# Routed experts of a two-layer block: the plain weight is loaded one slot later, and the vector engine's work inside a slot is put in another order

## The chip, the cores and the metric

The kernel runs on one core of a Trainium2 chip. The metric is the device time of one execution in microseconds; the time before is the median of three runs. TensorE (PE) does the matrix products, VectorE (DVE) and ScalarE (ACT) the element-wise work, GpSimd (POOL) and SyncE (SP) mostly start transfers (DMAs).

## The reference, cut to what matters

Two layers work on 4096 tokens of width 256. The second ends with a routed feed-forward block of 8 experts, and beside it with a mixture of four linear scans whose weights come from the top two of four gate logits (a rank, a top value and a sigmoid for each token):

```python
top_idx = jnp.argmax(gate_logits, axis=-1)
for e in range(NUM_EXPERTS):                       # 8 experts, D_FF = 1024
    mask = (top_idx == e)[..., None]
    h = relu(x @ w1[e] + b1[e])
    y = h @ w2[e] + b2[e]
    out = out + mask * y
...
top_vals, top_idx = jax.lax.top_k(x @ gate_W, 2)   # weights of the scan mixture
weights = softmax(top_vals)
```

The change touches only how this routed block, and the ranks of the last mixture, are put in order.

## The kernel before, in words

Products are made of float32 numbers split into a rounded high part and a low part: `mm3` does three products (high by high, high by low, low by high). Every operand therefore needs a high part (ACT, a copy in the rounded type) and a low part (DVE, a subtraction).

Tokens are sorted by expert into blocks of 128 rows in DRAM. The routed stage then runs over 23 slots in 8 rounds. A round has three slots, k = 0, 1 and 2: two "big" ones of 256 rows with split weights, and a "small" one of 128 rows (`small(k)`), whose first layer takes the plain float32 weight `w1_small` and the plain rows `sT_small`. The last round has only the two big slots. Round 0 and round 7 are written out, rounds 1 to 6 are a hardware loop. Below, slot (r, k) is slot k of round r.

What each engine does in a slot n:

- PE: layer 1 (`L393` to `L395` in a big slot, `L1581` in a small one) fills four PSUM banks q = 0..3, two of the eight column blocks in each; then layer 2 (`L1597` to `L1599`) sums over j = 0..7. Layer 2 waits, for each pair of j, for the low part `eT_l` of that pair (`e_ok`), at j = 0 and 4 for the halves of the low part of w2 (`w2_lo`), and at its start for `ys_ok`, that is, until the sums of the slot before have been taken out of PSUM. Layer 1 of a small slot waits for both halves of `w1_small` (`w1s_in`).
- ACT: for each q, `relu` (two instructions, L1675) and `round_e` (the high part, L1683); between them the high parts of the weights (`w1_half` L1652, `w2_half` L1659) and of the rows (L1663).
- DVE, function `slot` at the end of the file: `rows_out` of the slot before (bias added, L2071; it waits for that slot's last matmul and for its bias `b2b`), `low_e` for each q (L2062), the low parts of the weights (`w1_half` L2035, `w2_half` L2056) and of the rows (L2051), and the turning of the next rows (`turn_rows` L2045). In the first slot of the last round it also has, behind each `low_e`, one `mixture_rank` (L500 to L506), and at the end of the last slot `mixture_top` (L513 to L517) and `mixture_finish`.
- SP, function `slot` of the first block: a queue, in program order, of `store_y` (L1413), the second half of the next w2 (`raw2_half`, L1399, issued when DVE has made the low part of the half that is overwritten), `load_b2` (L1417), in slot 0 of rounds 1 to 6 both halves of `w1_small` (`load_w1_small`, L1392), `load_b1` (L1407), the next w1 (`raw1_half`, L1385, also behind the low parts; both halves in k = 0, one in k = 1 and one in k = 2), and the first half of the w2 after the next. The raw weights have one buffer each.
- POOL loads the rows of later slots (L1811), on a queue of its own.

Of the kernel before, what the change touches and what calls it, by code (L numbers as in the profile page):

```python
# [44 lines left out]
ST = SLOT // P  # L45
# [3 lines left out]
ROUND = 3  # L49
# [15 lines left out]
def build(nc, a, out):  # L65
# [484 lines left out]
    def zero(g):  # L550
        return isinstance(g, int) and g == 0
# [119 lines left out]
    def left(r, k):  # L671

        return NSLOT - 1 - ROUND * r - k if isinstance(r, int) else NSLOT
# [10 lines left out]
    with nc.Block("all") as block:  # L684
# [626 lines left out]
        def _(sp):  # L1311
# [76 lines left out]
            def load_w1_small(r, e):  # L1388
                if not zero(r):
                    wait_alone(sp, l1_full, FJ // 2 * ROUND * r)  # L1390
                for h in (0, 1):
                    sp.dma_start(w1_small[:, :, h * HALF1:(h + 1) * HALF1],  # L1392
                                 a["w1"][bass.ds(e, 1), h].rearrange("a p c f -> p (a c) f")).then_inc(w1s_in, 16)
# [8 lines left out]
            def load_b1(n, k, e):  # L1402
                if not (isinstance(n, int) and n < ROUND):
                    wait_alone(sp, t_ok, FJ * (n - ROUND + 1))
                if not zero(n):
                    wait_alone(sp, b1_in, 16 * n)
                sp.dma_start(b1c[:, k % ROUND, :], a["b1"][bass.ds(e, 1)].rearrange("a p j -> p (a j)")).then_inc(b1_in, 16)  # L1407

            def store_y(r, k):

                wait_alone(sp, ys_ok, ROUND * r + k + 1)
                b, st = blocks(r, k)
                sp.dma_start(y_v[bass.ds(b, st)].rearrange("b p d -> p b d"), y_sb[:, 0:st, :]).then_inc(y_st, 16)  # L1413

            def load_b2(e):

                sp.dma_start(b2b[:], a["b2"][bass.ds(e, 1)].to_broadcast((P, D))).then_inc(b2_in, 16)  # L1417
# [3 lines left out]
            def expert_at(r, o):  # L1421

                if o not in ahead:
                    ahead[o] = expert(ROUND * r + o)
                return ahead[o]

            def slot(r, k):

                n = ROUND * r + k
                if k == 0:  # L1430
                    ahead.clear()
                if not zero(n):
                    store_y(*((r, k - 1) if k else (r - 1, ROUND - 1)))
                if left(r, k) > 0:
                    raw2_half(n + 1, 1, expert_at(r, k + 1))
                load_b2(expert_at(r, k))
                if left(r, k) > 1 and k == 0 and not zero(r):
                    load_w1_small(r, expert_at(r, ST))
                if left(r, k) > 1:
                    load_b1(n + 2, k + 2, expert_at(r, k + 2))  # L1440
                if not small(k) and bigs_left(r, k) > 1:
                    e = expert_at(r, k + ROUND)
                    raw1_half(bigs(r, k) + ST, 0, e)
                    if k == 0:
                        raw1_half(bigs(r, k) + ST, 1, e)
                if small(k):
                    raw1_half(bigs(r, k - 1) + ST, 1, expert_at(r, k - 1 + ROUND))
                if left(r, k) > 1:
                    raw2_half(n + 2, 0, expert_at(r, k + 2))
# [385 lines left out]
        def _(dve):  # L1835
# [238 lines left out]
            def first_halves():  # L2074
# [7 lines left out]
                low_e(0, 3, SLOT)  # L2082
                w1_half(1, 0)

            def low_halves(r, k):

                n, (_, st) = ROUND * r + k, blocks(r, k)
                for q in range(FJ // 2):
                    low_e(n, q, st * P)
                    if left(r, k) == 1:  # L2090
                        mixture_rank(dve, link, mix2, q)
                    if q == 2 and not small(k):
                        for ahead in range(k + 1, next_big(k) + 1):
                            if left(r, k) > 0:
                                turn_rows(r, ahead)
                    if q == 0 and k == 0:
                        w2_half(n, 1)
                    if q == (2 if k == 0 else 1) and not small(k) and bigs_left(r, k) > 0:
                        w1_half(bigs(r, k) + 1, 0)

            def slot(r, k):
                n, (_, st) = ROUND * r + k, blocks(r, k)
                if not zero(n):
                    rows_out(*((r, k - 1) if k else (r - 1, ROUND - 1)))
                if not zero(n) and k > 0:
                    w2_half(n, 1)
                if zero(n):
                    first_halves()
                else:
                    low_halves(r, k)  # L2110
                if left(r, k) > 0:
                    if not small(k):
                        rows_lo(r, next_big(k))
                    if not small(k) and bigs_left(r, k) > 0:
                        w1_half(bigs(r, k) + 1, 1)
                    w2_half(n + 1, 0)
                if left(r, k) == 0:
                    mixture_top(dve, link, mix2)
                    mixture_finish(dve, link, mix2, 2)

            g = GROUPS - 1
# [86 lines left out]
```

## Time and profile before

| | |
|---|---|
| median of 3 runs | 1025.59 us (1025.57 to 1028.11) |
| the profiled execution | 1028.48 us, of which the span is 1026.8 us |
| routed stage, on PE | 645.40 to 881.44 us of the span, 236.0 us |
| granted PE clock | 1.00 |

The span is what the profile covers, from the first to the last instruction; all times of rows are from its start.

### The profile page before, as it was taken

The page shows a single profiled execution, that of the slowest core. Times are in us where ns is not written, and L with a number is a line of the kernel's source. Part 1 is how long each engine was busy: PE and PEld are TensorE (multiplying, and loading weights), DVE is VectorE, ACT ScalarE, POOL GpSimd, SP SyncE. Part 2 cuts the span into 40 slices and gives each one's busy share as a digit, 9 for nine tenths or more (in the row PEclk, how much of TensorE's full clock was granted, in tenths as well). Part 3 has the DMA queues.
Part 4 walks back from the last instruction along what each step waited for, and adds up shares of the span by engine and source line. Part 5 has one row for each costly group of instructions (what it writes and reads, how often), then busy time and mean ns, then how long its engine had stood idle before and what let it go on. Part 6 is the DMA issues. An engine that isn't in the chain of part 4 may idle for free.

```text
span 1026.8 us, 20067 instructions
## 1 busy us (share of the span) xinstructions
PE 1016.7 (99%) x6432; PEld 908.7 (88%) x6432; DVE 793.2 (77%) x1307; ACT 626.2 (61%) x1179; POOL 373.9 (36%) x376
## 2 busy tenths in 40 slices
PE   8999999999999999999999999999999999999998
PEld 7988989989898988989877888999999999888887
DVE  6876767667685777969789998977788778588887
ACT  4554445535444454555566667888889888566665
POOL 3443443444444453443552775122122110482000
PEclk9999999999999999999999999999999999999999
DMA  6226313122132221442546376688897885652203
GB/s 190 69 83 221 103 41 82 55 79 70 41 82 82 81 82 62 144 165 63 194 157 245 116 286 221 199 249 250 267 286 249 284 262 182 230 178 68 92 11 102
DMA packets 112130, 152.12 MB, mean 148 GB/s; under 512 B 40720, under 2 KB 80656, under 8 KB 111056
## 3 DMA queue, kind: packets, MB, share of 16 engines
q1 hardware_dynamic: 100368, 132.35, 39.3%
q0 software_dynamic: 6016, 13.51, 4.5%
q10 hardware_dynamic: 5696, 5.64, 1.7%
q8 instruction: 26, 0.43, 0.2%
q14 instruction: 24, 0.20, 0.1%
HBM read 109.20 MB, written 42.27 MB: 148 GB/s over the span
## 4 chain that ended last, share of the span: by engine, by line
PE 86%; DVE 4%; DMA 3%; issue 3%; SPq 2%; ACT 2%; DVEq 0%; POOL 0%; ACTq 0%; POOLq 0%
PE ps L395 17%; PE ps L393 17%; PE ps L394 17%; PE ps L1194 6%; PE ps L1195 6%; PE ps L1196 6%; DMA raw<-w 2%; PE ps L1597 2%; PE ps L1598 2%; PE ps L1599 2%; PE ps L1212 2%; PE ps L1213 2%; PE ps L1214 2%; PE ps L1263 1%; PE ps L1256 1%
## 5 line engine op out<-in xcount | busy, mean ns | idle before, releaser
L827 POOL TENSOR_TENSOR acc<-acc,ytmp 128x512 f32<-128x512 f32 x120 | 157.7, 1314 | 243.3 <-ACT ytmp L918 223.4
L1637 ACT ACTIVATE act_o<-ps,scan_bias 128x512 f32<-128x512 f32 x189 | 129.5, 688 | 98.1 <-PE ps L395 94.1
L918 ACT ACTIVATE ytmp<-ps,sel 128x256 f32<-128x256 f32 x256 | 107.3, 471 | 95.7 <-PE ps L1196 95.1
L995 DVE SCALAR_TENSOR_TENSOR hT_l<-ps,hT_h 128x512 fp32r<-128x512 f32 (+1 forms) x136 | 88.4, 655 | 87.7 <-ACT hT_h L878 87.6
L1194 PE MATMUL ps<-vals_h,hT_h 128*128 128x256 f32 x512 | 144.9, 283 | 0.1
L1195 PE MATMUL ps<-vals_l,hT_h 128*128 128x256 f32 x512 | 143.8, 281 | 0.0
L1196 PE MATMUL ps<-vals_h,hT_l 128*128 128x256 f32 x512 | 143.5, 280 | 0.0
L878 ACT ACTIVATE hT_h<-ps 128x512 fp32r<-128x512 f32 x128 | 76.3, 596 | 89.4 <-PE ps L395 84.9
L1811 POOL DMA_DIRECT2D rows<-xs_d x92 | 52.8, 575 | 175.2 <-DVE sT L2045 163.8
L1980 DVE TENSOR_TENSOR_SCAN h_b<-a_b,hstate,xs_b 128x512 f32<-128x512 f32 x63 | 88.1, 1398 | 28.2 <-ACT a_b L1644 24.8
L1040 DVE SCALAR_TENSOR_TENSOR acc<-ps,sel,acc 128x256 f32<-128x256 f32 x240 | 104.0, 475 | 3.0 <-PE ps L1196 2.9
L1194 PEld LDWEIGHTS ps<-vals_h,hT_h 128*128 128x128 f32 x512 | 96.5, 188 | 6.4 <-issue 0.8
L1195 PEld LDWEIGHTS ps<-vals_l,hT_h 128*128 128x128 f32 x512 | 96.2, 188 | 4.6
L1196 PEld LDWEIGHTS ps<-vals_h,hT_l 128*128 128x128 f32 x512 | 97.0, 189 | 0.0
L393 PE MATMUL ps<-xT_h,keys_h 128*128 128x512 f32 x240 | 96.7, 403 | 0.0
L395 PE MATMUL ps<-xT_h,keys_l 128*128 128x512 f32 x240 | 94.9, 395 | 0.0
L394 PE MATMUL ps<-xT_l,keys_h 128*128 128x512 f32 x240 | 94.7, 395 | 0.0
L1597 PE MATMUL ps<-w_h,eT_h 128*128 128x256 f32 x312 | 89.8, 288 | 3.9 <-DVE eT_l L2062 3.0
L1598 PE MATMUL ps<-w_l,eT_h 128*128 128x256 f32 x312 | 88.1, 282 | 0.0
L1599 PE MATMUL ps<-w_h,eT_l 128*128 128x256 f32 x312 | 87.9, 282 | 0.0
L395 PE MATMUL ps<-x1T,WB_late 128*128 128x512 f32 (+2 forms) x198 | 77.6, 392 | 0.0
L1675 ACT ACTIVATE t<-ps,b1c 128x256 f32<-128x256 f32 (+1 forms) x184 | 70.0, 431 | 11.1 <-DMA b1c<-b 6.9
(261 smaller groups left out, 2769.6 us busy)
## 6 DMA issues: line engine op xcount, KB each, us to landing
raw<-w SPq DMA_DIRECT2D x78, 512.0 KB, 5.4
x1T<-xT_d SPq DMA_DIRECT2D x16, 512.0 KB, 5.5
comb_b<-comb_d SPq DMA_DIRECT2D x8, 1024.0 KB, 8.5
xn_d<-xn SPq DMA_DIRECT2D x15, 512.0 KB, 2.9
w_small<-w SPq DMA_DIRECT2D x14, 512.0 KB, 5.1
xs_d<-zeros ACTq DMA_DIRECT2D x1, 4992.0 KB, 19.5
x_d<-x SPq DMA_DIRECT2D x8, 512.0 KB, 4.5
xT_d<-nT_h SPq DMA_DIRECT2D x8, 512.0 KB, 2.7
```

Source lines behind the costliest of these rows:

```text
L393: pe.matmul(dst, wh, xh, start=start, stop=False)
L394: pe.matmul(dst, wh, xl, start=False, stop=False)
L395: return pe.matmul(dst, wl, xh, start=False, stop=stop)
L827: pool.tensor_tensor(dst[:, 2:4, :], acc[:, 2:4, :], ytmp[:, k % 2, :, :], ALU.add).then_inc(acc23, 1)
L918: act.activation(ytmp[:, k % 2, j - 2, :], yb(k, j), ACT.Copy, scale=sel[:, j, k:k + 1]).then_inc(y_23, 1)
L1194: pe.matmul(yb(k, j), hT_h[:, k % 2, s], vals_h[:, k, :], start=True, stop=False)
L1195: pe.matmul(yb(k, j), hT_h[:, k % 2, s], vals_l[:, k, :], start=False, stop=False)
L1196: last_mm = pe.matmul(yb(k, j), hT_l[:, k % 2, s], vals_h[:, k, :], start=False, stop=True)
L1597: pe.matmul(dst, eT_h[:, j, t], w2_h[:, j, :], start=j == 0, stop=False)
L1598: pe.matmul(dst, eT_h[:, j, t], w2_l[:, j, :], start=False, stop=False)
L1599: last_mm = pe.matmul(dst, eT_l[:, j, t], w2_h[:, j, :], start=False, stop=j == FJ - 1)
L1637: act.activation(act_o[:, i % 2, w, :], ps[:, 3 * (i % 2) + w, :], func, bias=scan_bias[:, w, i:i + 1]).then_inc(act_g, 1)
```

## The change

In the queue of SP: the plain weight `w1_small` is loaded in slot k = 1 of rounds 1 to 6, behind `load_b1`, and no longer in slot k = 0; in a small slot `load_b2` comes ahead of the second half of w2, in the big slots it stays behind it. On DVE: in slots k = 0 the sums of the slot before (`rows_out`) are taken out behind the first `low_e`, no longer ahead of it; in small slots `w2_half(n, 1)` comes behind the first `low_e`, no longer ahead of it. The four `mixture_rank` of the last mixture move from slot (7, 0) to the slots (0, 1) (behind its last `low_e`) and (0, 2) (behind its last three), and `mixture_top` from the end of slot (7, 1) to the end of slot (0, 2).

```diff
@@ -1431,13 +1431,16 @@
                     ahead.clear()
                 if not zero(n):
                     store_y(*((r, k - 1) if k else (r - 1, ROUND - 1)))
+                if small(k):
+                    load_b2(expert_at(r, k))
                 if left(r, k) > 0:
                     raw2_half(n + 1, 1, expert_at(r, k + 1))
-                load_b2(expert_at(r, k))
-                if left(r, k) > 1 and k == 0 and not zero(r):
-                    load_w1_small(r, expert_at(r, ST))
+                if not small(k):
+                    load_b2(expert_at(r, k))
                 if left(r, k) > 1:
                     load_b1(n + 2, k + 2, expert_at(r, k + 2))
+                if left(r, k) > 0 and k == 1 and not zero(r):
+                    load_w1_small(r, expert_at(r, ST))
                 if not small(k) and bigs_left(r, k) > 1:
                     e = expert_at(r, k + ROUND)
                     raw1_half(bigs(r, k) + ST, 0, e)
@@ -2082,27 +2085,31 @@
                 low_e(0, 3, SLOT)
                 w1_half(1, 0)
 
+            RANKS2 = [(1, 3), (2, 1), (2, 2), (2, 3)]
+
             def low_halves(r, k):
 
                 n, (_, st) = ROUND * r + k, blocks(r, k)
                 for q in range(FJ // 2):
                     low_e(n, q, st * P)
-                    if left(r, k) == 1:
-                        mixture_rank(dve, link, mix2, q)
+                    if zero(r) and (k, q) in RANKS2:
+                        mixture_rank(dve, link, mix2, RANKS2.index((k, q)))
                     if q == 2 and not small(k):
                         for ahead in range(k + 1, next_big(k) + 1):
                             if left(r, k) > 0:
                                 turn_rows(r, ahead)
                     if q == 0 and k == 0:
+                        rows_out(r - 1, ROUND - 1)
+                    if q == 0 and k != 1:
                         w2_half(n, 1)
                     if q == (2 if k == 0 else 1) and not small(k) and bigs_left(r, k) > 0:
                         w1_half(bigs(r, k) + 1, 0)
 
             def slot(r, k):
                 n, (_, st) = ROUND * r + k, blocks(r, k)
-                if not zero(n):
-                    rows_out(*((r, k - 1) if k else (r - 1, ROUND - 1)))
                 if not zero(n) and k > 0:
+                    rows_out(r, k - 1)
+                if k == 1:
                     w2_half(n, 1)
                 if zero(n):
                     first_halves()
@@ -2114,8 +2121,9 @@
                     if not small(k) and bigs_left(r, k) > 0:
                         w1_half(bigs(r, k) + 1, 1)
                     w2_half(n + 1, 0)
+                if zero(r) and small(k):
+                    mixture_top(dve, link, mix2)
                 if left(r, k) == 0:
-                    mixture_top(dve, link, mix2)
                     mixture_finish(dve, link, mix2, 2)
```

## Rows read from the trace of the kernel before

**Rows 1.** The page: busy time by engine, and the chain by engine.

```profile
PE 1016.7 (99%) x6432; PEld 908.7 (88%) x6432; DVE 793.2 (77%) x1307; ACT 626.2 (61%) x1179; POOL 373.9 (36%) x376
...
PE 86%; DVE 4%; DMA 3%; issue 3%; SPq 2%; ACT 2%; DVEq 0%; POOL 0%; ACTq 0%; POOLq 0%
```

**Rows 2.** Busy time by stretch: slot k = 1 of rounds 1, 3, 5.

```profile
687.04:700.14 13.10, 11.71 (x99) 11.51 (x97) 9.21 (x13) 9.91 (x18) 1.93 (x4) 1.00 0.90 287
...
749.12:760.50 11.38, 11.38 (x98) 11.38 (x97) 9.92 (x14) 10.20 (x18) 2.76 (x5) 1.00 0.97 319
...
809.14:820.59 11.45, 11.45 (x99) 11.45 (x98) 9.45 (x13) 10.16 (x18) 2.17 (x4) 1.00 0.97 327
```

**Rows 3.** Busy time by stretch: slot k = 2 of rounds 0, 1; sum of all seven.

```profile
668.36:675.34 6.98, 6.69 (x58) 6.53 (x57) 5.11 (x8) 5.38 (x15) 2.51 (x5) 1.00 0.73 206
700.14:707.16 7.02, 6.71 (x59) 6.52 (x57) 5.10 (x8) 5.06 (x14) 2.74 (x5) 1.00 0.71 199
...
sum 48.49, PE 47.19 PEld 45.73 DVE 34.76 ACT 38.63 POOL 15.95; mean PE 6.74 PEld 6.53 DVE 4.96 ACT 5.52 POOL 2.28
```

**Rows 4.** Busy time by stretch: slot k = 0 of rounds 5, 6, 7.

```profile
797.44:809.14 11.70, 11.70 (x99) 11.52 (x98) 8.52 (x11) 9.99 (x18) 2.21 (x4) 1.00 0.78 249
827.37:839.37 12.00, 11.72 (x99) 11.51 (x97) 8.49 (x11) 10.48 (x18) 2.21 (x4) 1.00 0.74 243
857.64:870.05 12.41, 11.65 (x98) 11.45 (x97) 10.37 (x24) 9.93 (x17) 0.00 (x0) 1.00 0.56 174
```

**Rows 5.** PE in order of time: start, duration, line, idle before with releaser.

```profile
697.16 0.38 PE L1597 MATMUL ps<-w_h,eT_h 128*128 128x256 f32 x1 [1.39 <-DVE eT_l L2062]
...
704.19 0.38 PE L1597 MATMUL ps<-w_h,eT_h 128*128 128x256 f32 x1 [0.31 <-DVE eT_l L2062]
...
868.52 0.39 PE L1597 MATMUL ps<-w_h,eT_h 128*128 128x256 f32 x1 [0.76 <-DVE eT_l L2062]
```

**Rows 6.** ACT in order of time, slots (1, 1), (1, 2) and (6, 0).

```profile
693.86 1.06 ACT L1652 ACTIVATE w_h<-raw 128x1024 fp32r<-128x1024 f32 x1 [2.28 <-DMA raw<-w]
...
701.39 0.60 ACT L1675 ACTIVATE t<-ps,b1c 128x128 f32<-128x128 f32 x2
...
704.91 0.42 ACT L1683 ACTIVATE eT_h<-t 128x256 fp32r<-128x256 f32 x1
...
830.86 1.07 ACT L1659 ACTIVATE w_h<-raw 128x1024 fp32r<-128x1024 f32 x1 [0.19 <-DMA raw<-w]
```

**Rows 7.** SP's queue in order of time: the plain weight, w1, and three loads of b1.

```profile
683.65 2.74 SPq L1392 DMA_DIRECT2D w_small<-w  x2
...
688.27 1.43 SPq L1385 DMA_DIRECT2D raw<-w  x2
...
692.85 0.33 SPq L1407 DMA_DIRECT2D b1c<-b  x1
...
754.73 0.33 SPq L1407 DMA_DIRECT2D b1c<-b  x1
...
814.05 0.33 SPq L1407 DMA_DIRECT2D b1c<-b  x1
```

**Rows 8.** DMA issues at 692.87:692.97: size, us from issue to landing.

```profile
b1c<-b SPq DMA_DIRECT2D x1, 4.0 KB, 6.0
```

**Rows 9.** DMA issues at 754.75:754.85, the same columns.

```profile
b1c<-b SPq DMA_DIRECT2D x1, 4.0 KB, 7.1
```

**Rows 10.** DMA issues at 814.07:814.17, the same columns.

```profile
b1c<-b SPq DMA_DIRECT2D x1, 4.0 KB, 5.7
```

**Rows 11.** DVE in order of time: small slot (1, 2), and ranks in slot (7, 0).

```profile
702.50 1.22 DVE L2056 TENSOR_TENSOR w_l<-raw,w_h 128x1024 fp32r<-128x1024 f32 x1
703.63 1.19 DVE L2062 TENSOR_TENSOR eT_l<-t,eT_h 128x256 fp32r<-128x256 f32 x3
...
863.75 0.17 DVE L504 TENSOR_TENSOR cmp<-logits 128x8 f32<-128x8 f32 x1
...
864.60 0.69 DVE L2062 TENSOR_TENSOR eT_l<-t,eT_h 128x512 fp32r<-128x512 f32 x1
```

## The prediction

> **What bounds the kernel now.** I read the page first: PE is busy for 99% of the span and makes up 86% of the chain that ended last [rows 1]. So an edit to the order of DVE's and SP's work can only pay where PE stands still, or cost where it makes PE stand still. I then cut the routed stage into its slots and read each stretch by itself. PE works there at one matmul of 256 columns in about 0.118 us (rows 2: the second slot of round 5 has its 96 in 11.45 us, that of round 3 in 11.38 us, with PE busy all the way). At this rate a big slot is worth 11.4 us, and a small one 32 plain products of 0.11 us and 24 of 0.118 us, 6.4 us. The 23 slots would need 16 x 11.4 + 7 x 6.4 = 227 us and take 236. All that can be won in this stage is thus 9 us, 0.9% of the time, and the timeline says where it lies:
>
> - Slot (1, 1) takes 13.10 us, 1.7 over the floor [rows 2]. PE waits there for 1.39 us for `eT_l` in the middle of layer 2 [rows 5]; behind that wait is ACT, which stood for 2.28 us until the first half of w1 had landed [rows 6]. That half was issued at 688.27, behind two plain weight transfers whose issue at 683.65 took 2.74 us [rows 7].
> - The seven small slots take 48.5 us together, 3.7 over their floor, each between 6.8 and 7.1 [rows 3]. Layer 2 starts late, on `eT_l` [rows 5], because DVE first does the 1.22 us of `w2_half` and only then `low_e` [rows 11].
> - The slots k = 0 of rounds 1 to 5 take about 11.7 us, that of round 6 takes 12.00 and that of round 7 takes 12.41 [rows 4]; in the last PE waits for 0.76 us for an `eT_l` [rows 5] that stands behind the ranks of the mixture.
>
> The other view that matters is the DMA share, the column before the last of rows 2 to 4: 0.78 in the slot k = 0 of round 5, about 0.7 in small slots, but 0.97 in the slots k = 1 of rounds 3 and 5. The load that the change moves goes from the first of these stretches into the one that is full.
>
> **The change, part by part.**
>
> *The plain weight leaves slot 0.* Its two halves no longer stand ahead of b1 and of the first half of w1. In round 1 the w1 half can be issued some 3 us earlier (it then waits only for the low part of the old w1), so the 2.28 us of ACT [rows 6] and the stall they cause go: 13.10 to 11.6, **-1.5 us**. The slots k = 1 of the other rounds have no stall to lose: 0. The bounds are -1.6 and 0.
>
> *The plain weight enters slot 1.* Its landing must now come before the small slot starts, 11.4 us after the slot k = 1 began. How late is it? No row shows it in that place. The nearest is b1, which is then the transfer just ahead of it. It is issued 4.9 to 5.8 us after the slot's start and lands at 698.85, 761.83 and 819.75 in rounds 1, 3 and 5 [rows 7 to 10], that is 11.8, 12.7 and 10.6 us after the starts of their slots [rows 2]. These 4 KB take 5.7 to 7.1 us, so they wait behind the queue, and what is queued is served in about the order of issue. The queue had the 1 MB of the plain weight in it too, ahead; after the change the same bytes are served in another order, and the plain weight lands last, where b1 landed, plus what the DMA engines idle because the w1 half that now comes first has to wait for the low part of the old w1, and the plain weight had nothing to wait for (it had been free since the round before). Rows 7 bound this: it cannot be more than the 4.6 us between 683.65 and 688.27 and is far less, as b1 and most of the wait lie within them. I put it at 0.6 us, and at 1 us in round 1, where the queue was fullest. Then the landings are at 12.8, 13.3 and 11.2 us, against 11.4 us: late by 1.4, 1.9 and not at all. The other three loops, read in the same way, lie at 10.6 or below for b1, like round 5, and count as in time. Sum: **+3.2 us**. Bounds: 0 (all in time), and 12 (each late by 2 us, below).
>
> On this point a page would decide otherwise. The Trainium skill, "DMA: Bandwidth & Descriptors", section "Anatomy of one DMA — SWDGE (gpsimd) path", prices a transfer at about 2 us fixed plus its bytes at 436 GB/s. By this an estimate for a half of 512 KB is 3.2 us, the second half, issued some 6.4 us into the slot, lands at 9.6 us, no round is late, and this term is 0. The rows do not agree: 4 KB took 5.7 us or more [rows 8 to 10].
>
> *`low_e` ahead of `w2_half` in the small slots.* PE can start layer 2 some 0.3 us earlier, at the end of layer 1. What is late next is ACT: its first `relu` starts 1.25 us behind the slot's start (701.39 against 700.14) and its last `round_e` ends at 705.33, 5.19 us behind it [rows 3, 6]. Add DVE's 0.4 us for the low part [rows 11], 0.1 for the signal and the last six matmuls with their restart, 0.8, and the slot ends at 6.5 to 6.6. The six small slots of rounds 1 to 6 take 48.49 - 6.98 = 41.5 us now [rows 3]; six of 6.55 are 39.3: **-2.2 us**. `w2_half(n, 1)` is 0.4 us later and is needed 1.4 us into layer 2: hidden, but barely. Bounds: -2.5 and 0.
>
> *What hangs on it.* SP issues the second half of the next w2 only when this `w2_half` is done, so 0.4 us later, and now behind the 128 KB of b2, which take 0.4 us at the 327 GB/s of rows 2. ACT needs this half in the next slot k = 0 behind its first pair, and in round 6 it already waits for it for 0.19 us [rows 6]; every delay of ACT there passes on to PE, since all slots k = 0 are 0.3 over the floor on ACT's chain. With small slots that are 0.4 us shorter the need also comes earlier. I take 0.8 us in all (round 3 and round 6, 0.4 each). Bounds: 0 and 4 (0.65 in each of six).
>
> *b2 earlier, `rows_out` behind the first `low_e` in slots k = 0.* The same DVE work in another order; it matters only where b2 landed late. In round 6 this and the half w2 made 12.00 out of 11.7 [rows 4]: **-0.3 us**. Elsewhere ACT's chain hides it: 0. PE needs the sums taken out only at its layer 2, 5.7 us into the slot; `store_y` moves by under 1 us. Bounds -0.5 and +0.5.
>
> *The ranks.* Slot (7, 0) loses them: 12.41 to 11.7, **-0.7 us**. `mixture_top` at the end of (7, 1) had nothing of PE behind it: 0. In slot (0, 1) the first rank stands behind the last `low_e`: it moves the next slot's DVE work by about 0.1 us. In slot (0, 2) a rank of four instructions takes 0.85 us (863.75 to 864.60) [rows 11], and two of them stand between the last three `low_e` of 0.4 us; PE uses one pair in 0.7 us and waits for each next. DVE's chain from the first `low_e` is 0.4 + 1.1 + 0.4 + 0.85 + 0.4 + 0.85 + 0.4 = 4.4 us, and PE has 0.8 us left when it ends; the first can start 2.4 us into the slot. This gives 7.6 to 7.7 us for a slot that takes 6.98 [rows 3]: **+0.7 us**. `mixture_top` then fills a time in which DVE waits for a transfer: 0, and 0.85 without this cover. Bounds 0 and +1.5.
>
> **The sum.** -1.5 + 3.2 - 2.2 + 0.8 - 0.3 - 0.7 + 0.7 = 0.0 us. The profiled execution, 1028.48 us with a span of 1026.8, would keep its span; it lies 2.9 us above the median of the runs, and the same difference holds for the median: 1025.6 us.
>
> **The rivals.** A measurement of this kernel can tell about 0.3%, 3.1 us.
>
> 1. *The plain weight is in time in every round* (what the page says, worked out here from rows as a queue that is never behind by more than the 5 us between issue and need). Then the +3.2 falls away: -3.2 us, 1022.4. For it: four of six rounds have b1 landed 0.8 us or more before the need. Against it: the share of 0.97 [rows 2]. Chance 0.2.
> 2. *The plain weight is late in every round: slower.* The place is the start of layer 1 of the six small slots. From the second half of w1 on, 3.1 MB of weights, sums and bias and 0.5 MB of rows must pass before it has landed. At 327 GB/s [rows 2] this takes 11.0 us, and it cannot begin before some 2.4 us into the slot, so the landing is at 13.4, late by 2.0 us. Six times 2.0 in place of 3.2 gives +8.8 us, 1034.4. It makes the change slower than can be told apart as soon as the mean lateness is above 1.05 us. For it: round 3. Against it: b1 at 10.6 us in round 5 with the same bytes. Chance 0.16.
> 3. *ACT or the second half of w2 takes back what the small slots gain* (+2.2 or more, up to the bound of 4): +2 to +3 us, 1028. Chance 0.12.
> 4. *The new order does nothing anywhere,* because each small stall only moves to the next wait: only the ranks and round 1 remain, -1.5: 1024.1. This lies inside the forecast's own spread.
>
> The forecast itself, with 4, has 0.52. Together: faster by over 0.3% needs rival 1 and nothing else against it, 0.14; slower by over 0.3% comes from rival 2 and a part of 3, 0.18; within 0.3%, 0.68. The range reaches from rival 1 with a little of the bounds left, 1022.0, to a mean lateness of about 1.2 us, 1029.6; the likeliest case alone would be 1024 to 1027.5.
>
> **What the profile after would show.** PE's wait of 1.39 us in slot (1, 1) gone and that slot at 11.6 or less; small slots of rounds 1 to 6 at 6.5 to 6.6 from the first L1581; slot (7, 0) at 11.7; slot (0, 2) at 7.6 with waits for `eT_l` between its pairs; and, before the first L1581 of rounds 1 and 3, a new wait of 1 to 2 us on `w_small<-w`. Landings of `w_small` around 5 us from issue, where it is issued some 6 us into the slot, would refute the last; a wait there in all six rounds means rival 2. If slots k = 0 grow beyond 11.8 with ACT waiting for `raw<-w` at L1659, it is rival 3.

## The result and the profile after

The changed kernel takes 1035.26 us (median of four runs, 1031.94 to 1042.79), the kernel before on the same chip 1025.58 us: ratio 1.0091, 95% interval [1.0066, 1.0115]. That is slower, and outside the range given. It is rival 2: the plain weight is late in every round.

The profiled execution after took 1033.79 us, 5.3 more than that of before. All but 0.1 of it lies in the routed stage, from the first L393 to L540: 241.26 us in place of 236.04 (everything behind it takes 145.3 in both). By kind of slot:

| us | before | after | change | change forecast |
|---|---|---|---|---|
| slots k = 0, rounds 1 to 7 | 82.86 | 81.66 | -1.20 | -0.2 |
| slots k = 1, eight | 93.23 | 99.77 | +6.54 | +1.7 |
| small slots, seven | 48.49 | 48.37 | -0.12 | -1.5 |

The page of the kernel after, busy time and the chain by engine, beside [rows 1]:

```profile
PE 1018.0 (99%) x6432; PEld 909.5 (88%) x6432; DVE 792.7 (77%) x1307; ACT 627.3 (61%) x1179; POOL 374.0 (36%) x376
...
PE 90%; DMA 4%; DVE 3%; issue 2%; SPq 1%; ACT 0%; POOL 0%; DVEq 0%; POOLq 0%; ACTq 0%
```

The 99% of PE say nothing here: it is as busy as before and later. Busy time by stretch tells more (columns as in [rows 2]). In order: slots (0, 2), (1, 1), (1, 2), (2, 1), (3, 1), (4, 1), (4, 2), (5, 0), (5, 1), (6, 1) and (7, 0) of the kernel after, beside [rows 2 to 4]:

```profile
668.43:675.87 7.44, 7.04 (x58) 6.59 (x57) 6.21 (x19) 5.89 (x14) 1.77 (x4) 1.00 0.80 230
687.57:700.32 12.75, 11.61 (x99) 11.40 (x97) 11.24 (x15) 11.27 (x19) 3.17 (x6) 1.00 0.97 329
700.32:706.86 6.54, 6.54 (x56) 6.54 (x57) 3.16 (x6) 3.84 (x12) 1.49 (x3) 1.00 0.99 268
718.60:731.03 12.43, 11.62 (x98) 11.40 (x96) 10.93 (x14) 11.01 (x19) 2.92 (x6) 1.00 0.96 332
749.26:762.11 12.85, 11.56 (x99) 11.35 (x97) 11.38 (x15) 11.29 (x19) 3.81 (x7) 1.00 0.97 336
780.34:793.92 13.58, 11.55 (x99) 11.34 (x97) 11.67 (x15) 11.26 (x19) 2.95 (x6) 1.00 0.95 314
793.92:802.10 8.18, 8.18 (x56) 8.18 (x57) 2.99 (x6) 5.12 (x13) 1.75 (x3) 0.79 0.82 231
802.10:813.78 11.68, 11.68 (x99) 11.50 (x98) 8.39 (x11) 9.76 (x17) 2.20 (x4) 1.00 0.47 158
813.78:826.95 13.17, 11.56 (x99) 11.35 (x97) 11.67 (x15) 11.27 (x19) 3.68 (x7) 1.00 0.94 322
845.17:857.33 12.16, 11.62 (x98) 11.41 (x96) 10.65 (x14) 10.73 (x19) 2.34 (x4) 1.00 0.97 339
...
863.88:875.40 11.52, 11.52 (x99) 11.46 (x98) 8.42 (x11) 9.78 (x17) 0.00 (x0) 1.00 0.52 168
```

PE is busy for its 11.4 to 11.6 us in every slot k = 1 and idle for the rest. The waits of PE (total, times, longest) name the cause, and show that the waits for `eT_l` (3.0 us in five places before) are gone but for two:

```profile
PE ps L1584 <- DMA w_small<-w: 7.4, 6, 2.0
...
PE ps L1600 <- DVE eT_l L2065: 0.4, 2, 0.2
```

Look then at the DMA share, the column before the last. Slot (5, 0) moved 249 GB/s for 11.70 us before, 2.9 MB [rows 4]; now it moves 158 for 11.68 us, 1.85 MB. Of the 1 MB that left it, half went into slot (5, 1), 4.24 MB in place of 3.74, and a third into the small slot behind it, 1.70 in place of 1.36. In slot (5, 1) the share was 0.97 already [rows 2], and the slot got longer instead, until the weight had landed. In round 4 its second half was issued at 786.50, the second of these two, and landed 7.4 us later, at 793.9, where PE starts:

```profile
785.82 1.23 SPq L1392 DMA_DIRECT2D w_small<-w  x2
```

```profile
w_small<-w SPq DMA_DIRECT2D x1, 512.0 KB, 7.4
```

One stretch is of another kind. Slot (4, 2) has no idle time at all and takes 8.18 us. Below is PE in order of time at its start, and then stretches of 1 us before and in its layer 1, where the granted clock is the third column from the end:

```profile
793.92 5.47 PE L1584 MATMUL ps<-sT_small,w_small 128*128 128x128 f32 x32 [2.03 <-DMA w_small<-w]
```

```profile
792.00:793.00 1.00, 0.00 (x0) 0.00 (x0) 1.00 (x2) 0.98 (x1) 0.53 (x1) 1.00 1.21 332
794.00:795.00 1.00, 1.00 (x7) 1.00 (x8) 0.00 (x0) 0.00 (x0) 0.00 (x0) 0.79 1.04 266
795.00:796.00 1.00, 1.00 (x6) 1.00 (x6) 0.00 (x0) 0.54 (x2) 0.00 (x0) 0.50 0.95 246
796.00:797.00 1.00, 1.00 (x7) 1.00 (x6) 0.43 (x2) 0.50 (x2) 0.00 (x0) 0.50 1.00 315
...
798.00:799.00 1.00, 1.00 (x11) 1.00 (x11) 0.55 (x2) 0.71 (x3) 0.78 (x2) 1.00 0.12 40
```

Behind the longest of the six waits the granted clock went from 2.4 to 1.2 GHz for some 3 us, and layer 1 of this slot took 5.22 us where it takes 3.59 in the other rounds: 1.6 us on top of the wait.

### The profile page after: what moved, and what is told of

The parts are those of the page before. It is cut to its first block, busy times and chain, and to the rows that moved or that the text cites. A ratio compares the mean times of both kernels' runs of the same rounds, so it can differ in the third digit from the quotient of the medians.

```text
span 1032.1 us, 20068 instructions
## 1 busy us (share of the span) xinstructions
PE 1018.0 (99%) x6432; PEld 909.5 (88%) x6432; DVE 792.7 (77%) x1307; ACT 627.3 (61%) x1179; POOL 374.0 (36%) x376
## 4 chain that ended last, share of the span: by engine, by line
PE 90%; DMA 4%; DVE 3%; issue 2%; SPq 1%; ACT 0%; POOL 0%; DVEq 0%; POOLq 0%; ACTq 0%
PE ps L393 17%; PE ps L395 17%; PE ps L394 17%; PE ps L1194 6%; PE ps L1195 6%; PE ps L1196 6%; DMA w_small<-w 4%; PE ps L1600 3%; PE ps L1602 2%; PE ps L1601 2%; PE ps L1584 2%; PE ps L1212 2%; PE ps L1213 2%; PE ps L1214 2%; PE ps L1263 1%
## 5 line engine op out<-in xcount | busy, mean ns | idle before, releaser
L393 PE MATMUL ps<-xT_h,keys_h 128*128 128x512 f32 x240 | 96.7, 403 | 0.0
L2065 DVE TENSOR_TENSOR eT_l<-t,eT_h 128x512 fp32r<-128x512 f32 (+1 forms) x92 | 55.8, 606 | 43.5 <-ACT eT_h L1686 43.2
```

The source lines that it names most:

```text
L393: pe.matmul(dst, wh, xh, start=start, stop=False)
```

## The experiments

The theory of the result (A; the expectations call it Q): the six loads of 1 MB went into a stretch whose DMA engines were full, so any place with a gap undoes the loss. Its rivals: that the order of issue on SP, not the bytes, makes the weight late; that the loss is in ACT's chain behind the second half of w2; and, beside it, theory C, that the waits cost more by the clock than by themselves. On two of the chips the kernel before too took 1044 and 1051 us in place of 1026 or 1027. The traces taken there show PE idle for 9 to 30 us in all ahead of and behind the routed stage, where the kernel before on a chip without this has none, and a lower granted clock about these waits. The longest is this, from 921 to 940 us in the kernel with the ranks moved (described last):

```profile
PE ps L393 <- ACT act_o L1637: 19.2, 1, 19.2
```

So for runs there the length of the stage in the trace is compared, and the ratio is given for what it is worth. Two traces of one kernel differ by 0.7 and 0.9 us in this length (two kernels were traced twice); a difference of less between single traces says nothing.

**The load back in slot 0, all else as changed.**

```diff
+                if left(r, k) > 1 and k == 0 and not zero(r):      # ahead of load_b1
+                    load_w1_small(r, expert_at(r, ST))
-                if left(r, k) > 0 and k == 1 and not zero(r):      # behind load_b1
-                    load_w1_small(r, expert_at(r, ST))
```

> The changed kernel with the plain weight loaded in slot k = 0 again; the new order of DVE, the earlier b2 and the moved ranks stay. Theory Q (the late landing of the plain weight is the whole loss): its waits at layer 1 of the small slots go, the small slots of rounds 1 to 6 stay at 6.55 us and slot (7, 0) at 11.5 us as in the changed kernel's trace, slot (1, 1) has its stall of 1.4 us back. 2.2 + 0.9 us won against the kernel before, 0.5 us lost in slot (0, 2): about 1023 us. Rival V (the new order on DVE carries part of the loss): 1026 us or more, with slots k = 0 longer than 11.8 us.

Measured: 1032.17 us against 1027.30, ratio 1.0037 [1.0024, 1.0050], stage 241.30. No wait for the weight is left, the small slots take 6.44 to 6.55, and yet the stage is as long as that of the changed kernel. The 1023 us of theory Q were missed; the time and the slots k = 0 are those of rival V, but its cause, DVE's order, is not the one that the runs below show. The loss only moved. Waits of PE and ACT (this wait of ACT is 8.7 us in the kernel before), slot (2, 0) by stretch, and SP's queue ahead of it:

```profile
PE ps L1600 <- DVE eT_l L2065: 8.8, 14, 1.5
...
ACT w_h L1662 <- DMA raw<-w: 17.1, 13, 2.2
```

```profile
706.60:720.60 14.00, 11.93 (x99) 11.52 (x98) 8.72 (x11) 10.94 (x18) 2.21 (x4) 1.00 0.71 223
```

```profile
702.74 0.41 SPq L1413 DMA_DIRECT2D y_d<-y_sb  x1
703.34 0.34 SPq L1417 DMA_DIRECT2D b2b<-b  x1
704.11 0.33 SPq L1399 DMA_DIRECT2D raw<-w  x1
```

The slots k = 0 of rounds 2 to 6 take 12.7 to 14.0 us. ACT stands for the second half of w2, which is now issued behind b2: the rest of the change has a price that the late plain weight had covered. So there were two losses to tell apart.

**The load moved, all else as before.**

```diff
-                if left(r, k) > 1 and k == 0 and not zero(r):      # ahead of load_b1
-                    load_w1_small(r, expert_at(r, ST))
+                if k == 1 and not zero(r):                         # behind load_b1
+                    load_w1_small(r, expert_at(r, ST))
```

> The kernel before with only the load of the plain weight moved to slot k = 1. Theory Q: it has the whole loss and none of the gains, waits of 0.8 to 2.2 us before layer 1 in all six small slots, small slots of 7.0 us or more, slot (7, 0) at 12.4 us: 1035 to 1040 us, as slow as the changed kernel or slower by some 3 us. Rival V: under 1032 us, since the order on DVE is the old one.

Measured: 1033.02 us, ratio 1.0070 [1.0049, 1.0091], stage 238.88. PE waits in six places for 6.8 us:

```profile
PE ps L1581 <- DMA w_small<-w: 6.8, 6, 1.9
```

So the move alone makes the kernel slower, and the waits are its own. That was expected; small slots of 7.0 us and 1035 us or more were not met. The small slots take 6.55 us here with DVE's old order: while PE waits for the weight, DVE and ACT get ahead. Of the 2.2 us that the forecast gave to the new order, all comes with the wait for nothing, and the two cannot be added.

**The load between the two halves of w1 in slot 0.**

```diff
-                if left(r, k) > 0 and k == 1 and not zero(r):
-                    load_w1_small(r, expert_at(r, ST))
...
                     raw1_half(bigs(r, k) + ST, 0, e)
+                    if k == 0 and not zero(r):
+                        load_w1_small(r, expert_at(r, ST))
                     if k == 0:
                         raw1_half(bigs(r, k) + ST, 1, e)
```

> The changed kernel with the plain weight loaded in slot k = 0 between the two halves of w1, where SP waits for a low part anyway, so that it is ahead of neither b1 nor the first w1 half. Theory Q: it lands in the first half of slot k = 1, no wait before layer 1 of a small slot, no stall in slot (1, 1), the gains of the order on DVE stay: 1021 to 1022.5 us, faster than the kernel before by 0.3 to 0.4%. Rival (the DMA engines are the bound, wherever the load stands): the second half of w1 and the halves of w2 are late in its place and PE waits for w1_lo or w2_lo in slots k = 1: 1025 us or more.

Measured: 1026.06 us, ratio 0.9987 [0.9978, 0.9995], stage 232.80. No wait for the weight, all slots k = 1 at 11.38 to 11.46, slot (1, 1) too; small slots 6.44 to 6.61 from round 1 on. The loss of theory A and the old order's stall in (1, 1) are both gone, though the 1021 to 1022.5 us expected were missed. The slots k = 1 of rounds 1 to 6 moved 3.9 to 4.1 MB each here, at 342 to 357 GB/s, without getting longer; so the 327 GB/s at a share of 0.97 [rows 2] were not yet the most that such a slot can move, and the changed kernel asked for 4.1 to 4.3 MB, the weight last. In slots (3, 0) and (3, 1) by stretch is seen what is left, 0.6 us or so on `eT_l` in slots k = 0:

```profile
735.23:747.67 12.44, 11.86 (x99) 11.58 (x98) 8.62 (x11) 10.65 (x18) 1.80 (x4) 1.00 0.60 204
747.67:759.05 11.38, 11.38 (x98) 11.38 (x97) 9.91 (x14) 10.21 (x18) 2.76 (x5) 1.00 0.98 342
```

**Half of the bytes.**

```diff
-                    for h in (0, 1):
+                    for h in (0, 1) if zero(r) else (0,):   # load_w1_small
```

> The changed kernel with only the first half of the plain weight loaded in rounds 1 to 6 (the second half stays that of round 0, so the result is of mixed weights). 512 KB less of the 1 MB stand in slot k = 1. Theory Q (the load is late because the DMA engines are full there, share 0.94 to 0.97, and it is last in the queue): the one transfer lands some 1.4 us earlier than the second did, so waits of 0.8 to 2.2 us shrink to 0 to 0.8 us, 2 us in all or less, and the time is 1024 to 1027 us. Rival (the wait is for the issue, which SP reaches late, not for the bytes): the first half is issued where it was, and most of the waits stay, 1031 us or more.

Measured: 1042.57 us against 1044.39 on its chip, ratio 1.0044 [0.9998, 1.0089]; stage 234.85. The place in the queue is that of the change, the bytes are half, and on PE one wait is left, 1.3 us in round 1; the other slots k = 1 take 11.38 to 11.46, (0, 1) 11.79. It is the bytes, not the place of issue. And the price of b2 comes to light again, 12.3 to 12.4 us in the slots k = 0 of rounds 3, 4 and 6. The 1024 to 1027 us expected can't be compared, as this chip is one of the two.

**Matmuls that need no weight in the place of the wait: six, then three.**

```diff
+                if small(k) and not zero(r):
+                    for _ in range(6): pe.matmul(ps[:, 6, 0:D], ident[:], zeros[:], start=True, stop=True)
```

> The changed kernel with six matmuls of constants (256 columns, plain float32, into a bank that is not used there) ahead of layer 1 of the small slots of rounds 1 to 6; their result is not used. They fill the time in which PE waited for the plain weight. Theory C (beside the waits of 8.7 us the stalls cost the clock: the granted clock was 0.5 for 3.4 us behind the wait of 2.0 us in round 4, and the runs with a mean clock of 0.993 to 1.0 spread from 1031.9 to 1042.8 us): the clock stays at 1.00 in every run and the runs agree within 2 us, near 1032 us. Rival (the spread has to do with the landing times alone): the spread of some 10 us stays, and the mean clock below 1.

> As the kernel with six matmuls of constants ahead of the small slots, but with three; six took 2.59 us (slots k = 1 of 13.98 us), so three take 1.3 us. Theory C (the clock falls behind a long wait of PE): what is left of the waits is under 1 us, the clock is 1.00 in every run, the spread is that of the kernel before, about 3 us, and the time is 1031 to 1033 us, less than that of the changed kernel although PE has more work. Rival (the spread came with the landing times, not with the clock): a median of 1035 us or more, spread as in the changed kernel.

Six: 1039.24 us (1038.57 to 1040.63), ratio 1.0120 [1.0106, 1.0135], stage 245.97. They cost 2.6 us in each slot, more than I had put them at, so the expected time was missed; no wait is left, so in this kernel the weight is never 2.6 us late. The four runs lie within 2.1 us and have the full clock, where the four of the changed kernel spread over 10.9 us with mean clocks of 1.000, 0.998, 0.998 and 0.993 in the order of their times. That is in favour of theory C. But the clock does not carry the whole spread: one fall like the one above lowers the mean clock by 0.0016, so 0.993 stands for some four, and 4 x 1.6 = 6.4 us of the 10.9 us is an estimate of their part. Three: stage 245.36, on one of the two chips above, ratio 1.0106 [1.0032, 1.0180]. The weight came later yet in rounds 3 and 4; in round 3 a wait of 1.85 us was left, and layer 1 behind it took 5.22 us. The expectation failed, and the run neither removed the falls nor refutes them.

**b2 behind the second half of w2 again, on top of the load between the halves.**

```diff
-                if small(k):
-                    load_b2(expert_at(r, k))
                 if left(r, k) > 0:
                     raw2_half(n + 1, 1, expert_at(r, k + 1))
-                if not small(k):
-                    load_b2(expert_at(r, k))
+                load_b2(expert_at(r, k))
```

> The kernel with the plain weight between the halves of w1, and with b2 again behind the second half of w2 in small slots. Theory B (b2 ahead delays that half: in the kernel with the load put back, b2 landed 3.4 us behind the sums, and the half another 1.3 us behind it, while ACT waited 2.2 us for it): slots k = 0 of rounds 3, 4 and 6, now 12.1 to 12.4 us, fall to 11.7 to 11.9, 1 to 2 us less than with b2 ahead, some 2.5 us below the kernel before. Rival N (the need has come earlier since the small slots are 0.4 us shorter, and the order of the two transfers does not matter): no difference of more than 0.5 us, and ACT still waits for that half.

> The kernel with the plain weight between the halves of w1 and b2 behind the second half of w2, once more, since on the chip of the last call the stretches behind the routed stage ran at a lower clock, in the kernel before too. Its routed stage took 231.2 us there, against 236.0 us in the kernel before. On a chip without that: 4 to 5 us below the kernel before, a ratio of 0.995 to 0.996. If the ratio is over 0.998, a shorter routed stage is given back behind it.

First run: 1041.72 us, ratio 0.9992 [0.9931, 1.0054], stage 231.16; again on another chip: 1047.68, ratio 0.9955 [0.9926, 0.9984], stage 231.89 (one small slot took 7.63). In the first the slots k = 0 of rounds 1 to 6 are at 11.66 to 11.78. Against 232.80 with b2 ahead, the stage is 0.9 to 1.6 us shorter; the slots k = 0 of rounds 1 to 7 together fall from 83.65 to 81.66 and 81.70, so the order of the two transfers is worth 2.0 us there.

**DVE's part alone: loads and b2 as before.**

> The kernel before with only DVE's part of the change (order in the slots and ranks); all transfers in SP's old order. Theory B: the loss of 4.9 us that the kernel with the load put back showed goes, since it came from b2 ahead of the second half of w2: small slots 6.5 us, slots k = 0 of 11.7 to 12.3 us, 1025 to 1026 us with the kernel before at 1027.3 us. Rival N (earlier need of the half of w2, later issue behind the later w2_half of DVE): slots k = 0 stay at 12.6 to 14.0 us and the time at 1030 us or more.

> The kernel before with DVE's part alone, once more for the same reason. Its routed stage took 234.4 us, so 1.6 us below the kernel before is what is left, a ratio near 0.9985. If it is above 1.000, DVE's part is no gain on its own.

1046.69 us, ratio 1.0039 [0.9987, 1.0091], stage 234.44; and 1051.57, ratio 0.9989 [0.9967, 1.0011], stage 233.50. Small slots of rounds 1 to 6 are at 6.44 to 6.57, so the new order gives them by itself what the forecast said. The kernel of the first experiment differs from this one only in b2, and its stage is 241.30: 6.9 to 7.8 us for b2.

**b2 alone, on the kernel before.** And then the same with b2 read from 128 distinct rows in place of one row 128 times.

```diff
+                if small(k):
+                    load_b2(expert_at(r, k))
                 if left(r, k) > 0:
                     raw2_half(n + 1, 1, expert_at(r, k + 1))
-                load_b2(expert_at(r, k))
+                if not small(k):
+                    load_b2(expert_at(r, k))
```

```diff
-                sp.dma_start(b2b[:], a["b2"][bass.ds(e, 1)].to_broadcast((P, D)))
+                sp.dma_start(b2b[:], a["w2"][bass.ds(e, 1), 0, :, 0, :].rearrange("a p d -> p (a d)"))
```

> The kernel before with only b2 ahead of the second half of w2 in small slots. Theory B (b2 ahead delays that half, ACT gets it late in the next slot k = 0): slots k = 0 of rounds 1 to 6 grow from 11.7 us to 12 or more; since the small slots are still long and the half is issued 0.4 us earlier, less than the 6.9 us that the order of the two costs in the kernel with the load put back: 1 to 4 us in all. Rival: nothing (slots k = 0 at 11.7 us), then that cost needs the short small slots and the later issue with it.

> As the kernel with only b2 moved ahead in small slots, but b2b is filled with 128 different rows of w2 (128 KB, 1 KB for each partition) in place of one row of 1 KB read 128 times; the bias of the result is thus another. In that kernel b2 landed 3.2 us behind the sums and the half of w2 1.3 us behind it, and slots k = 0 of rounds 2 to 6 took 12.4 to 13.5 us. Theory R (it is the reading of one row 128 times that is slow when it stands alone in the queue): b2 lands under 1 us behind the sums, slots k = 0 fall to 11.7 to 12.0 us, the routed stage to 236 us. Rival P (place and number of the 1 KB packets matter, whatever they read): as in that kernel, 240 us.

One row: 1058.74 us, ratio 1.0050 [1.0014, 1.0086], stage 240.56, 4.5 more than before. The slots k = 0 of rounds 1 to 7 take 89.81 in place of 82.86, 7.0 more (12.4 to 13.5 in rounds 2 to 6); the slots k = 1 and the small slots take 2.4 less, and no run says whether that is b2 or the scatter of traces. Distinct rows, on another chip: 1028.93 us, ratio 1.0015 [1.0006, 1.0025], stage 236.36, 0.3 more than before; slots k = 0 of rounds 1 to 7 84.57, 1.7 more, with 12.0 to 12.4 in rounds 2, 4, 5 and 6, where at most 12.0 had been expected. The waits of ACT for the half, with the one row and then with distinct rows (8.7 us before):

```profile
ACT w_h L1662 <- DMA raw<-w: 15.2, 13, 1.7
```

```profile
ACT w_h L1662 <- DMA raw<-w: 9.3, 10, 1.7
```

SP's queue at these two loads (b2 and the half of w2) in round 3, and their size and time from issue to landing, first with the one row:

```profile
771.32 0.34 SPq L1417 DMA_DIRECT2D b2b<-b  x1
771.90 0.33 SPq L1399 DMA_DIRECT2D raw<-w  x1
```

```profile
b2b<-b SPq DMA_DIRECT2D x1, 128.0 KB, 7.1
...
raw<-w SPq DMA_DIRECT2D x1, 512.0 KB, 7.8
```

And with distinct rows:

```profile
762.09 0.42 SPq L1417 DMA_DIRECT2D b2b<-w  x1
762.76 0.33 SPq L1399 DMA_DIRECT2D raw<-w  x1
```

```profile
b2b<-w SPq DMA_DIRECT2D x1, 128.0 KB, 5.9
...
raw<-w SPq DMA_DIRECT2D x1, 512.0 KB, 6.6
```

The 256 KB of y, the transfer ahead of b2, landed at 775.2 and at 766.8, b2 at 771.32 + 7.1 = 778.4 and at 762.09 + 5.9 = 768.0. So the same 128 KB land 3.2 us behind it when they are one row of HBM read 128 times, and 1.2 us behind it when they are 128 rows; the half of w2 behind them takes 6.6 us in place of 7.8. Round 3 is one of seven. Read in the same way, b2 landed behind y by:

| us, small slot of round | 0 | 1 | 2 | 3 | 4 | 5 | 6 |
|---|---|---|---|---|---|---|---|
| one row, kernel before with b2 ahead | 1.1 | 2.4 | 2.6 | 3.2 | 2.8 | 3.5 | 2.0 |
| distinct rows, the same kernel | 0.3 | 2.4 | 0.6 | 1.2 | 0.6 | 2.2 | 0.7 |
| one row, the changed kernel | 0.3 | 0.5 | 1.0 | 0.6 | 0.3 | 0.5 | 0.3 |

In the slots k = 1 of both kernels, where b2 stands behind a half of w2 in the full queue, it landed 0.3 to 0.4 us behind that half, one row or 128. So one row is not slow everywhere, and why it is where the queue is short no run says: the 384 packets of 1 KB of y and b2 in the round shown took 56 ns each in the mean with the one row and 54 with distinct rows. What the pair shows, with one trace each, is that most of b2's price hangs on how it is read and not on its bytes: 5.2 of the 7.0 us in the slots k = 0. The ratios, 1.0050 and 1.0015, point the same way, but their intervals overlap. The forecast had priced it at its bytes, 0.4 us.

**The changed kernel with b2 back alone.**

> The changed kernel with only b2 put back behind the second half of w2 in small slots; the plain weight stays in slot k = 1. Theory Q (in the changed kernel the wait for the plain weight is what PE sees, and it hides the late half of w2): the waits before layer 1 of the small slots stay, 1 to 2 us in each of six rounds, slots k = 0 stay at 11.7 us, and the routed stage is within 1.5 us of the 241.3 us of the changed kernel. Rival (the early b2 is also why the plain weight is late): the waits shrink by half or more, the stage is under 238 us.

1035.56 us, ratio 1.0069 [1.0043, 1.0096], stage 245.72, 4.5 over that of the changed kernel where 1.5 at most had been expected. The six waits for the plain weight stay, and the slots k = 0 are at 11.7:

```profile
PE ps L1581 <- DMA w_small<-w: 11.9, 6, 4.0
```

So b2's place is not what makes it late, and putting b2 back wins nothing as long as PE stands for the weight. The wait of 4.0 us in round 1, where the changed kernel has 1.14, was not expected. SP issued the weight at 693.26 and 693.95 there, at 693.10 and 693.78 in the changed kernel, so it isn't late for its issue; it took longer to land, 9.3 us in place of 6.5 for the second half, in a slot that moved fewer bytes per us than the 329 GB/s above:

```profile
687.67:703.31 15.64, 11.62 (x98) 11.41 (x97) 11.68 (x15) 11.29 (x19) 4.67 (x8) 1.00 0.92 286
```

What slowed it no run says. Behind the wait the clock fell as in slot (4, 2) above (layer 1: 5.16 us).

**The ranks elsewhere.** All three of the round's ranks behind the last low part of slot (0, 2); and, in a second kernel, one behind each low part of (7, 1), so that no slot but the last carries any.

```diff
-            RANKS2 = [(1, 3), (2, 1), (2, 2), (2, 3)]
+            RANKS2 = {(1, 3): [0], (2, 3): [1, 2, 3]}
```

```diff
+                    if left(r, k) == 0: mixture_rank(dve, link, mix2, q)   # mixture_top behind them, as before
```

> As e7r, with the last three ranks all behind the last low part of slot (0, 2), none between them. PE no longer waits between its pairs: slot (0, 2) falls from 7.43 to 6.5 us and the time by 0.9 us against e7r. Rival: the next slot's low parts are late instead, since DVE does 2.1 us of ranks and 0.85 us of the top values in a row there, and slot (1, 0) grows beyond 11.7 us by as much.

> As e7r, but with one rank behind each low part of the last slot (7, 1), and the top values at its end as in the kernel before. No slot of round 0 holds a rank, DVE is idle 0.7 us before each low part of (7, 1), where PE uses one pair in 1.4 us. Slot (0, 2) falls from 7.4 to 6.5 us, slots (1, 0), (7, 0) and (7, 1) stay at 11.7, 11.5 and 11.4 to 11.7 us, the routed stage at 230.2 to 230.5 us, 5.6 us below the kernel before. Rival: the chain of ranks, top values, sigmoids and mixture ends later than the last matmul of (7, 1), and PE waits before the transpose of the mixture: up to 1 us given back.

First: 1049.16 us, ratio 0.9973 [0.9948, 0.9998], stage 230.95; slot (0, 2) falls to 6.58 us but (1, 0) rises to 12.46: moved, not won. Second: 1023.64 us (1022.91 to 1024.13) against 1027.27, ratio 0.9967 [0.9954, 0.9979], stage 230.49. This is the best version: it beats the kernel before by 0.33%, where the changed one is 0.91% behind it. Slots (0, 2), (2, 0), (2, 1) and (3, 2) by stretch:

```profile
668.21:674.76 6.55, 6.55 (x59) 6.52 (x57) 5.07 (x8) 5.09 (x14) 2.47 (x5) 1.00 0.64 182
704.37:716.06 11.69, 11.69 (x98) 11.51 (x97) 8.55 (x11) 10.37 (x18) 2.21 (x4) 1.00 0.67 203
716.06:727.51 11.45, 11.45 (x98) 11.45 (x97) 9.94 (x14) 10.22 (x18) 2.35 (x4) 1.00 0.98 353
757.09:763.54 6.45, 6.45 (x58) 6.45 (x57) 4.46 (x7) 5.43 (x14) 2.34 (x4) 1.00 0.96 281
```

PE is idle in none of them. The slots k = 1 of rounds 1 to 6 still run at shares of 0.97 to 1.00, but nothing is late there.

## Why the prediction was wrong

- **The plain weight leaves slot 0 (-1.5): right, but sized from one trace.** The wait for `eT_l` in slot (1, 1) is gone; without the new wait of 1.14 us the slot takes 12.75 - 1.14 = 11.61 us, as forecast. The stall is not in every execution, though: in the six traces with the weight in its old place the slot takes 13.10, 12.63, 11.78, 12.93, 11.82 and 11.46 us. With the weight moved no trace has it.
- **The plain weight enters slot 1 (+3.2): this step failed.** The eight slots k = 1 take 99.77 us, 8.7 over their floor of 8 x 11.38, and 7.4 of this are waits for the weight in all six rounds (0.55 to 2.03). I had put the landing where b1 had landed in the kernel before, plus 0.6 us in which the DMA engines idle (1 us in round 1), and so counted four rounds as in time. The second half of the weight landed, in us into the slot:

  | round | 1 | 2 | 3 | 4 | 5 | 6 |
  |---|---|---|---|---|---|---|
  | b1, kernel before | 11.9 | 10.6 | 12.7 | 9.9 | 10.6 | 10.2 |
  | second half of the weight, changed kernel | 12.7 | 12.4 | 12.8 | 13.5 | 13.1 | 12.1 |
  | difference | 0.8 | 1.8 | 0.1 | 3.6 | 2.5 | 1.9 |

  The rounds 1 and 3, forecast at 12.8 and 13.3, came about so; the four counted as in time did not, and the 0.6 us are 1.8 in the mean. "The same bytes are served in another order" would hold if the queue never ran dry. But slot 0, which had 1 MB less to move, then ran at a share of 0.47 to 0.58 in place of 0.71 to 0.82, and the capacity left there was lost. b1's landing in the trace of before told how long the queue was with that MB ahead of it; it did not tell that the MB could start later at no cost. Rival 2, which counted the bytes to pass and the rate, gave 13.4 us and 1034.4; the mean of the six is 12.8. It has the mechanism right; that its time lies within 1 us of the measured one is in part luck, as it put the waits at 12 us in place of 7.4 and had neither the clock nor the difference between medians and profiled executions, both below. The move alone (ratio 1.0070), half the bytes (one wait left) and the load in a gap (no wait, 0.9987) show this cause. The Trainium skill, "DMA: Bandwidth & Descriptors", section "Anatomy of one DMA — SWDGE (gpsimd) path", has a sum of a fixed part and the bytes, given there for transfers started by GpSimd, that puts a half at 3.2 us as an estimate. It is not borne out for these loads, which SP starts into a full queue: from issue to landing the first halves took 5.2 to 5.6 us and the second, for which PE waits, 5.9 to 7.4.
- **A term that was missing (+1.6).** Layer 1 of round 4 ran at a granted clock of 0.5 behind its wait. It makes the small slots 48.37 where the forecast had 47.0 and is most of the difference there. No wait in the kernel before brings the clock down in this stage, and I had not asked what a long one would do.
- **`low_e` ahead of `w2_half` (-2.2): right in size.** The small slots behind rounds 1 to 6 take 6.54 to 6.56 but for that one. The cause is shown by DVE's part alone (6.44 to 6.57). In the changed kernel itself it wins nothing of its own, since the wait would have given the same.
- **b2 and the second half of w2 (+0.8): mis-sized, and hidden.** Slots k = 0 of rounds 1 to 5 took 11.67 to 11.74 us, so the term was 0 here. By itself it is 4.5 us of the stage, above its own upper bound of 4, and 7.0 us of the slots k = 0; 6.9 to 7.8 of the stage with shorter small slots. Rival 3 described it, but as something that would add to the others. It cannot while the small slot begins late.
- **b2 earlier (-0.3) and the ranks (-0.7, +0.7): right.** Slot (6, 0) takes 11.67 us, slot (7, 0) 11.52, and slot (0, 2) 7.44 with the forecast's waits between its pairs (0.2 us each in two places). The price of the ranks there is rather 0.9 us, as the slot takes 6.55 without any (the last experiment); the 6.98 of the kernel before, from which the forecast counted, were 6.55 in another trace with the same instructions up to there (the load moved alone).

The three terms off are +5.5 (8.7 in place of 3.2), +1.6 and -0.8, together +6.3. The trace has +5.2 where the sum said 0: the slots k = 1 had 2.2 us over their floor to lose (93.23 - 91.04), not 1.5, and slots (7, 0) and (0, 2) did 0.2 each better. The medians differ by 9.7: the changed kernel's median lies 1.5 above its profiled execution, and that of before 2.9 below its own. The first fits the clock in part, as its slower runs have the lower mean clock. Where the second comes from, no trace shows; a candidate is that the traced execution of the kernel before had the large stall in slot (1, 1) and the longer slot (0, 2), which some other traces don't have.

## What to carry to other kernels

Before a transfer is moved, count the bytes per stretch of the schedule, and not only their order: here the move out of a stretch with a DMA share of 0.8 into one of 0.97 made the first idle and the second grow. A term that is hidden by another loss is not gone: price each part of a change with the others taken back, as here a loss of 7 us stood behind one of the same size. And when a fix removes one wait without effect on the time, look which wait took its place before the theory is given up. A stall that is to be won back should be seen in more than one trace.

## What the runs showed of the hardware

- A load of 128 KB that reads one row of 1 KB in HBM for all 128 partitions landed 1.1 to 3.5 us behind the sums ahead of it in seven small slots (3.2 in round 3); the same bytes from 128 rows landed 0.3 to 2.4 us behind them (1.2 in round 3). In the full queue of the slots k = 1 both landed 0.3 to 0.4 us behind the half of w2 ahead of them.
- Within the routed stage the granted clock fell to 0.5 behind idle times of PE of 1.85, 2.03 and 4.02 us, and not behind those of 1.61, 1.62, 1.81, 1.88 and 1.93 us; each fall cost about 1.6 us in layer 1 of the small slot. So the length of the wait alone doesn't decide; what does is open.
- On two chips the kernel before took 1044 and 1051 us in place of 1026 or 1027. In the traces taken there PE stood for ACT outside the routed stage, for 19.2 us at a stretch in one, with a granted clock of 0.66 from 920 to 940 us, and for 9.1 in another, with 0.77. In the first PE was idle from 921 us on, and the clock was 0.75 from 923 to 930 us and 0.50 from 930 to 940: the wait came first. ACT stood before that for up to 9.1 us for something that the profile doesn't name. Why this is so on these chips stays open.
